# All layer norms of an eight-layer kernel: in two halves with loops written out, and every fourth tile normalised by ScalarE

## What is computed

```
def _layernorm(x, axis=-1, eps=1e-05):
    m = jnp.mean(x, axis=axis, keepdims=True)
    v = jnp.var(x, axis=axis, keepdims=True)
    return (x - m) / jnp.sqrt(v + eps)

x = x + _L0_attn_ref(_layernorm(x, axis=-1), ...)   # delta net
x = x + _L0_ffn_ref(_layernorm(x, axis=-1), ...)    # sine feed-forward
...                                                 # six more of this form
x = x + _L3_ffn_ref(_layernorm(x, axis=-1), ...)    # routed experts
```

## Time and profile before

| | |
|---|---|
| median of 3 runs | 3606.04 us (3604.13 to 3606.18) |
| the profiled execution | 3612.15 us, span 3610.3 us |
| busy share of the span | TensorE 69%, VectorE 50%, ScalarE 36%, GpSimd 20% |
| mean granted clock of TensorE | 0.771 of full speed |

### The profile page before, as it was taken

The page is one execution under the profiler, slowest core; times in us unless marked ns, Lnnn a source line. Parts: engine busy times, 40 slices in busy tenths (PEclk is TensorE's granted clock), DMA queues, the critical chain, the costliest instruction groups (busy, mean ns, idle before and its releaser), DMA issues.

```text
span 3610.3 us, 65131 instructions
## 1 busy us (share of the span) xinstructions
PE 2505.6 (69%) x20692; PEld 1381.9 (38%) x20744; DVE 1809.9 (50%) x3541; ACT 1295.6 (36%) x2627; POOL 717.2 (20%) x1299
## 2 busy tenths in 40 slices
PE   2330695767676766675499999544898998988954
PEld 1220463445455545342234444331333333333433
DVE  2115255642222222366366666354777777777353
ACT  1111010522222221101156566322666666666512
POOL 3551132024444444002001111010000000000012
PEclk8565555867777686686599999665999999999766
DMA  1122421000000000000411110005111111111000
GB/s 30 42 53 49 98 61 40 0 6 0 0 0 0 0 0 0 7 0 13 143 28 30 27 27 22 3 16 139 29 29 31 27 31 30 28 31 27 10 14 23
DMA packets 129382, 103.26 MB, mean 29 GB/s; under 512 B 52254, under 2 KB 108967, under 8 KB 129002
## 3 DMA queue, kind: packets, MB, share of 16 engines
q1 hardware_dynamic: 129258, 101.55, 10.9%
HBM read 58.96 MB, written 41.94 MB: 28 GB/s over the span
## 4 chain that ended last, share of the span: by engine, by line
PE 50%; DVE 16%; POOL 11%; issue 11%; SPq 4%; ACT 4%; DVEq 2%; DMA 1%; POOLq 0%; ACTq 0%; PEldq 0%
PE psum L1811 9%; PE psum L1823 7%; PE psum L1800 6%; PE psum L1835 5%; SPq L1737 3%; DVE ba_blockmax L2029 2%; DVE X L1195 2%; PE psum L586 1%; POOL dn_ss L745 1%; POOL dn_vscale L746 1%; PE psum L1341 1%; PE psum L1328 1%; PE psum L1359 1%; PE psum L382 1%; ACT ba_pt L1899 1%
## 5 line engine op out<-in xcount | busy, mean ns | idle before, releaser
L2029 DVE TENSOR_REDUCE ba_blockmax<-psum 128x16 f32<-128x1024 f32 x512 | 609.2, 1221 | 200.3 <-PE psum L1800 196.9
L1899 ACT ACTIVATE ba_pt<-psum 128x512 f32<-128x512 f32 x1024 | 542.1, 601 | 286.5 <-PE psum L1811 286.4
L1800 PE MATMUL psum<-ba_ks,ba_qs 64*128 64x512 bf16 x1024 | 362.8, 433 | 45.4 <-DMA ba_ks<-ba_kstk 31.1
L1811 PE MATMUL psum<-ba_qs,ba_ks 64*128 64x512 bf16 x1024 | 335.4, 403 | 82.9 <-DVEq L59 51.5
L2031 DVE TENSOR_REDUCE sa_negmax<-psum 128x1 f32<-128x1024 f32 x256 | 304.5, 1221 | 164.6 <-PE psum L1800 164.2
L1899 ACT ACTIVATE sa_pt<-psum 128x512 f32<-128x512 f32 x512 | 268.7, 602 | 201.0 <-PE psum L1811 124.2
L1823 PE MATMUL psum<-ba_pt,ba_vh 128*32 128x512 f32 x2048 | 306.1, 673 | 0.0
L1800 PE MATMUL psum<-sa_ks,sa_qs 96*128 96x512 bf16 x512 | 200.1, 396 | 52.0 <-DMA sa_ks<-sa_kstk 31.3
L1811 PEld LDWEIGHTS psum<-ba_qs,ba_ks 64*128 64x128 bf16 x1024 | 80.2, 95 | 394.9 <-issue 366.0
L1811 PE MATMUL psum<-sa_qs,sa_ks 128*128 128x512 bf16 x460 | 175.4, 385 | 22.0 <-DVEq L59 19.4
L1942 POOL CAST ba_mparts<-ba_negmax 128x8 bf16<-128x8 f32 x64 | 12.2, 191 | 821.5 <-DVE ba_negmax L2044 821.5
(11 more groups left out here) (468 smaller groups left out, 4543.8 us busy)
## 6 DMA issues: line engine op xcount, KB each, us to landing
ba_qs<-ba_qstk SPq DMA_DIRECT2D x128, 96.0 KB, 2.1
ba_ks<-ba_kstk SPq DMA_DIRECT2D x128, 96.0 KB, 2.2
sa_qstk<-sa_pq SPq DMA_DIRECT2D x48, 128.0 KB
sa_kstk<-sa_pk SPq DMA_DIRECT2D x48, 128.0 KB
sa_qs<-sa_qstk SPq DMA_DIRECT2D x32, 192.0 KB, 2.6
sa_ks<-sa_kstk SPq DMA_DIRECT2D x32, 192.0 KB, 2.7
ba_qstk<-ba_pq SPq DMA_DIRECT2D x48, 128.0 KB, 2.3
ba_kstk<-ba_pk SPq DMA_DIRECT2D x48, 128.0 KB, 2.3
```

Of the source, the lines that this page charges most:

```text
L1800: last = nc.tensor.matmul(bank(2 * slot + h), qs[b][0:KP, :].rearrange("p (a r) -> p r a", r=NTB)[:, r, :], ks[b][0:KP, h * HALF:(h + 1) * ...
L1811: nc.tensor.matmul(bank(4 + slot), ks[b][K0:P, x_ * P:(x_ + 1) * P], qs[b][K0:P, h * HALF:(h + 1) * HALF], start=True, stop=True).then_inc ...
L1899: nc.scalar.activation(pt[2 * x_ + h][:, :], bank(4 + slot), ACT.Exp, scale=SCALE).then_inc(pt_in, 1)
L2029: ins = nc.vector.tensor_reduce(blockmax[g][:, r, :], src.rearrange("p (n s) -> p n s", s=BLOCK), AXX, ALU.max, negate=True)
```

## The change

Only layer_norm is changed. The 32 tiles are treated as two halves of 16: VectorE takes statistics, aggregates and adds EPS for one half, tells GpSimd, and goes on with the other; GpSimd computes a power of 16 columns for each half (twice each in sa). All loops of the norm over tiles and groups, on VectorE, TensorE and ScalarE, are written out, with constant addresses. In front of groups 0 and 4 VectorE waits for the root of the half and computes shift = -mean * rstd for it. Of each group VectorE normalises three tiles and ScalarE the fourth, as Identity with scale rstd and bias shift, one group ahead of its copies. TensorE waits for each tile of VectorE by itself (ready) and for ScalarE's (ready_a).

```diff
--- before.py
+++ after.py
@@ -120,6 +120,8 @@
     nc = k.nc
     tag = f"{tag}_norm"
     ready = [k.sem(f"{tag}_ready{g}") for g in range(2)]
+    ready_a = [k.sem(f"{tag}_ready_a{g}") for g in range(2)]
+    shift_in = k.sem(f"{tag}_shift_in")
     turned = [k.free_sem(f"{tag}_turned{g}") for g in range(2)]
     written = [k.free_sem(f"{tag}_xt{g}") for g in range(2)]
     var_in, root_out = k.sem(f"{tag}_var"), k.sem(f"{tag}_root")
@@ -131,71 +133,92 @@
     root = k.sb(f"{tag}_root_buf", [P, NT], ctx=ctx)
     rstd = k.sb(f"{tag}_rs", [P, NT], ctx=ctx)
     tmp = k.sb(f"{tag}_ln_tmp", [P, 2, NT], ctx=ctx)
+    shift = k.sb(f"{tag}_shift", [P, NT], ctx=ctx)
+    MINE = GROUP - 1
     layer = k.layers
+    halves = [slice(h * NT // 2, (h + 1) * NT // 2) for h in range(2)]
 
     def vector(v):
         k.start(v, layer)
         c = Chain(v, own)
-        with v.Fori(0, NT // 8) as i:
-            for n in range(8):
-                c.do(nc.vector.bn_stats(stats[:, bass.ds(i * 8 + n, 1), :], k.X[:, bass.ds(i * 8 + n, 1), :]))
-            c.restart()
-        for n in range(NT):
-            c.do(nc.vector.bn_aggr(mv[:, n, :], stats[:, n, :]))
-        c.sync()
-        nc.vector.tensor_scalar(tmp[:, 0, :], mv[:, :, 1], EPS, None, ALU.add).then_inc(var_in, 1)
-        v.wait_ge(root_out, 1)
+        for at in halves:
+            for n in range(at.start, at.stop):
+                c.do(nc.vector.bn_stats(stats[:, n, :], k.X[:, n, :]))
+            c.sync()
+            for n in range(at.start, at.stop):
+                c.do(nc.vector.bn_aggr(mv[:, n, :], stats[:, n, :]))
+            c.sync()
+            nc.vector.tensor_scalar(tmp[:, 0, at], mv[:, at, 1], EPS, None, ALU.add).then_inc(var_in, 1)
         if twice:
-            c.step(nc.vector.tensor_tensor(tmp[:, 0, :], rstd[:, :], rstd[:, :], ALU.mult))
-            c.step(nc.vector.tensor_tensor(tmp[:, 1, :], tmp[:, 0, :], mv[:, :, 1], ALU.mult))
-            nc.vector.tensor_scalar(tmp[:, 0, :], tmp[:, 1, :], EPS, None, ALU.add).then_inc(var_in, 1)
-            v.wait_ge(root_out, 2)
-            c.step(nc.vector.tensor_tensor(rstd[:, :], rstd[:, :], root[:, :], ALU.mult))
+            for h, at in enumerate(halves):
+                v.wait_ge(root_out, h + 1)
+                c.step(nc.vector.tensor_tensor(tmp[:, 0, at], rstd[:, at], rstd[:, at], ALU.mult))
+                c.step(nc.vector.tensor_tensor(tmp[:, 1, at], tmp[:, 0, at], mv[:, at, 1], ALU.mult))
+                nc.vector.tensor_scalar(tmp[:, 0, at], tmp[:, 1, at], EPS, None, ALU.add).then_inc(var_in, 1)
+        for g in range(NG):
+            i, z = g // 2, g % 2
+            if g % (NG // 2) == 0:
+                h = 2 * g // NG
+                v.wait_ge(root_out, (3 if twice else 1) + h)
+                if twice:
+                    c.step(nc.vector.tensor_tensor(rstd[:, halves[h]], rstd[:, halves[h]], root[:, halves[h]], ALU.mult))
+                if twice:
+                    v.wait_ge(own, c.n)
+                nc.vector.scalar_tensor_tensor(shift[:, halves[h]], mv[:, halves[h], 0], -1.0, rstd[:, halves[h]], ALU.mult,
+                                               ALU.mult).then_inc(shift_in, 1)
+            v.wait_ge(turned[z], i + 1)
+            for n in range(MINE):
+                t = g * GROUP + n
+                nc.vector.tensor_scalar(xn[z][:, n, :], k.X[:, t, :], mv[:, t, 0:1], rstd[:, t:t + 1],
+                                        ALU.subtract, ALU.mult).then_inc(ready[z], 1)
         c.restart()
-        with v.Fori(0, NG // 2) as i:
-            for g in range(2):
-                v.wait_ge(turned[g], i + 1)
-                for n in range(GROUP):
-                    t = i * 2 * GROUP + g * GROUP + n
-                    last = nc.vector.tensor_scalar(xn[g][:, n, :], k.X[:, bass.ds(t, 1), :], mv[:, bass.ds(t, 1), 0],
-                                                   rstd[:, bass.ds(t, 1)], ALU.subtract, ALU.mult)
-                    if n < GROUP - 1:
-                        c.do(last)
-                c.sync()
-                last.then_inc(ready[g], 1)
-            c.restart()
 
     def tensor(t):
         k.start(t, layer)
-        with t.Fori(0, NG // 2) as i:
-            for g in range(2):
-                t.wait_ge(ready[g], i + 1)
-                t.wait_ge(written[g], i + 1)
-                for n in range(GROUP):
-                    last = nc.tensor.transpose(k.psum[:, g, n * P:(n + 1) * P], xn[g][:, n, :], k.ident[:, :])
-                last.then_inc(turned[g], 1)
+        for g in range(NG):
+            i, z = g // 2, g % 2
+            t.wait_ge(written[z], i + 1)
+            for n in range(GROUP):
+                if n < MINE:
+                    t.wait_ge(ready[z], MINE * i + n + 1)
+                else:
+                    t.wait_ge(ready_a[z], i + 1)
+                last = nc.tensor.transpose(k.psum[:, z, n * P:(n + 1) * P], xn[z][:, n, :], k.ident[:, :])
+            last.then_inc(turned[z], 1)
 
     def scalar(a):
         k.start(a, layer)
         if affine_in is not None:
             a.wait_ge(*affine_in)
-        with a.Fori(0, NG // 2) as i:
-            for g in range(2):
-                a.wait_ge(turned[g], i + 2)
-                dst = k.XT[:, bass.ds(i * 2 * GT + g * GT, GT)]
-                if place is not None:
-                    nc.scalar.copy(place(i, g), k.psum[:, g, :].rearrange("p (c t) -> p c t", t=P // B)).then_inc(written[g], 1)
-                elif affine is None:
-                    nc.scalar.copy(dst, k.psum[:, g, :]).then_inc(written[g], 1)
-                else:
-                    nc.scalar.activation(dst, k.psum[:, g, :], ACT.Identity, scale=affine[0],
-                                         bias=affine[1]).then_inc(written[g], 1)
+
+        def normalise(g):
+            i, z = g // 2, g % 2
+            t = g * GROUP + MINE
+            a.wait_ge(shift_in, 1 + 2 * g // NG)
+            a.wait_ge(turned[z], i + 1)
+            nc.scalar.activation(xn[z][:, MINE, :], k.X[:, t, :], ACT.Identity, scale=rstd[:, t:t + 1],
+                                 bias=shift[:, t:t + 1]).then_inc(ready_a[z], 1)
+
+        normalise(0)
+        for g in range(NG):
+            i, z = g // 2, g % 2
+            if g < NG - 1:
+                normalise(g + 1)
+            a.wait_ge(turned[z], i + 2)
+            dst = k.XT[:, g * GT:(g + 1) * GT]
+            if place is not None:
+                nc.scalar.copy(place(i, z), k.psum[:, z, :].rearrange("p (c t) -> p c t", t=P // B)).then_inc(written[z], 1)
+            elif affine is None:
+                nc.scalar.copy(dst, k.psum[:, z, :]).then_inc(written[z], 1)
+            else:
+                nc.scalar.activation(dst, k.psum[:, z, :], ACT.Identity, scale=affine[0], bias=affine[1]).then_inc(written[z], 1)
 
     def gpsimd(p):
         k.start(p, layer)
         for q in range(2 if twice else 1):
-            p.wait_ge(var_in, q + 1)
-            nc.gpsimd.tensor_tensor((root if q else rstd)[:, :], tmp[:, 0, :], k.mhalf[:, 0:NT], ALU.pow).then_inc(root_out, 1)
+            for h, at in enumerate(halves):
+                p.wait_ge(var_in, 2 * q + h + 1)
+                nc.gpsimd.tensor_tensor((root if q else rstd)[:, at], tmp[:, 0, at], k.mhalf[:, 0:NT // 2], ALU.pow).then_inc(root_out, 1)
 
     k.add(vector=vector, tensor=tensor, scalar=scalar, gpsimd=gpsimd)
     return written
```

## The result

| | before | after |
|---|---|---|
| median | 3606.11 us (3604.13 to 3615.8, 4 runs) | 3471.18 us (3468.66 to 3473.79, 4 runs) |
| profiled execution, span | 3612.15, 3610.3 us | 3468.66, 3466.8 us |
| busy TensorE, VectorE, ScalarE, GpSimd | 69, 50, 36, 20% | 72, 51, 38, 21% |

The account below looks back on a forecast made before the run. No engine bounds the kernel; the eight layer norms, 272.03 us, lie fully on the path as successive stages. Savings of 79.7 (six norms), 13.6 (ba) and 11.9 (sa) sum to 105.2 us off the median 3606.04: 3501 us, range 3486 to 3533.

Parts of the forecast that it names:

- Statistics written out: VectorE's statistics in each norm, without loops: 4.62 us a half, 9.24 us for both halves.
- A power doesn't hold VectorE's tiles: VectorE writes tiles beside GpSimd's second power without delay; waiting for that power's end would cost 2.9 us a norm.
- The cover: Second power lies under the first groups' tiles; groups 4 to 7 suffer only if its root comes after 13.1 us or so.
- The tiles' period: Tiles, transposes and copies on three engines: 1.0 us a group, between 0.92 and today's 1.54.
- dn's one table load: dn's norm loads ScalarE's table once, not on four passes, 1.28 us a load; group 0 is delayed by 0.8 us.
- sa: sa's norm: groups after 0 to 2 wait until memsets end at 24.9 us; 32.2 us long, 11.9 less.
- I take the later stages to run as now … some us either way: Stages behind the norms keep their times and are costed at nothing, though TensorE's granted clock changes behind the norms.
- the prediction's own last sign of being wrong: Stretches between the norms that differ from today's by more than some us would show the prediction wrong.
- ba: ba's norm: memsets interleave with tiles over groups 3 to 7, 2.5 us more; 21.25 us long, 13.6 saved.
- Rival 3: Moved code makes other loops' restarts dearer; 3523 us at 0.5 us a pass; chance 0.03 slower, 0.02 the same.
- Rival 2: Tiles don't speed up: semaphores round three engines keep 1.45 us a group in eight norms; 3526 us, chance 0.13.
- Rival 1: A GpSimd power holds VectorE's tiles: six norms lose 2.9 us each, sa and ba save less; 3528 us, chance 0.22.

Follow-up runs that it names:

- extra_power: Changed kernel with one more 16-column power on a spare tile in GpSimd's queue ahead of the last power; 3498.33 us, ratio 0.9677.
- before_again: The kernel before the change, unedited, run and profiled again on the experiments' chips; 3613.32 us, ratio 0.9998.
- after_again: The changed kernel, unedited, run and profiled again, against the kernel before on the same chip; 3473.80 us, ratio 0.9604.

## Why the forecast was wrong, step by step

| step | forecast | measured |
|---|---|---|
| first tile after the first bn_stats | 9.45 | 9.10 |
| first tile to end of the last copy | 9.3 | 8.08 |
| six norms together save | 79.7 | 89.3 |
| ba saves | 13.6 | 15.0 |
| sa saves | 11.9 | 17.3 |
| between the norms | 0 | 21.9 |
| sum | 105.2 | 143.5 |

The last column is the difference of the two profiled executions (3612.15 and 3468.66). One was 6 over its median, the other 2.5 under, so the medians give 134.9, and 139.0 in the later pair. Of the 21.9, 0.3 lies ahead of dn's first bn_stats.

The mechanism was right, and no rival came true. Three terms of the sum failed: the tiles' period, taken as 1.0; sa's second half, let wait for the memsets' end; and the later stages, put at nothing. The norms saved 16.4 us more than forecast, and the low end had allowed for 8.5; the rest of the program gave 13 by the medians, and it had allowed for 6. So about 8 of the 15 us under the range are the norms' and 7 the later stages'.

- *Statistics written out*: right, 4.62 a half forecast and 4.61 measured, and the first power at 4.78, the second at 9.19 against 4.8 and 9.4. The rest of the 0.35 is that shift and tile each start 0.08 us behind the instruction ahead, not 0.2.
- *A power doesn't hold VectorE's tiles*: right, and shown (twelve tiles in 3.35 us, nearly all of it beside a power of 3.06). L885 was the right row to go by, and it told more than I read in it: by the same section of the Trainium skill a form with two inputs in SBUF contends with GpSimd work that reads SBUF, as a power does, and its 0.35 us inside the power was its usual time (0.352 is the median of 32). The Trainium skill's rule (SBUF — State Buffer, Who interferes with whom), by which the first tiles would end at 12.35, doesn't fit the power. It fits the memsets where the two engines take turns (no tile over 1.2 us); a hung tile waited for the whole row of ten or eleven memsets, not for one.
- *The cover*: my limit of 13.1 was too late. At 12.25 there is at most 0.2 us of slack, as extra_power shows. Here it cost nothing.
- *The tiles' period*: this term failed. The floor of 0.88 for ScalarE, from the copy, the pointer operands and the SBUF source, was exact: 0.88, with a tile of 0.49 to 0.50. I took 1.0 instead, with no engine's work behind it. The last group is quicker still, since no tile stands between the last two copies (1.11 us for both). Together 1.2 us a norm, 7.3 in six.
- *dn's one table load*: right; 1.28 us ahead of ScalarE's first tile, and the norm 1.0 longer than the others (18.13).
- *sa*: what failed is "the rest I let wait to the end, as this layer shows it today". The row is of a tile that came behind a memset. In the changed kernel the tiles come first. 26.77 is near the 28.2 that I had for turns.
- *"I take the later stages to run as now … some us either way"*: this term failed, and the prediction's own last sign of being wrong came true. Stretches that the diff doesn't touch gave 13 us by the medians, 21.9 in the first pair of profiles and 15.4 in the second (before_again and after_again): 9.1 and 7.7 from dn's to sf's norm, 5.0 and 3.3 in ba's own stretch, 2.8 and 2.6 in tt's. Of dn's, 5.0 and 6.0 are TensorE's stalls between instructions. 1.0 is the four products right behind dn's norm, 1.13 us in all nine kernels written out where they took 2.10 in the four with loops. The other 1 to 3 have no cause that I could show. The 1.8 and 1.7 that sf's and rf's stretches gave in the first pair didn't repeat (-1.0 and -0.2). sf's follows the granted clock over it: 101.9 us at 0.90 of full speed, 105.8 at 0.82, 110.0 at 0.78.
- *ba*: near, but not by the interleaving alone: its norm is 34.84 or 38.16 us before and 19.83 or 24.39 after, so the saving is 10 to 18 by which executions are compared.
- *Rival 3* had the right place, code that moves, and the wrong sign; its mechanism, dearer loop passes, no run shows. *Rival 2* is out: 0.83 to 0.99 us a group on the mean of a plain norm in all kernels written out but extra_power, which has one long gap. *Rival 1* would have cost 3.1 a plain norm, and 24 to 27 us in all.

Left open: why some stretches gain. tt's is 713.7 to 714.3 us long in the four profiles with loops in the norm and 710.8 to 713.3 in the nine without, ba's 1025.0 to 1025.3 and 1015.9 to 1023.3. Their granted clock is the same (0.73 to 0.76, and 0.86 to 0.88, over both kinds), so it isn't the clock. Open, too, is why a tile that comes first hangs in some executions.

## What to carry to other kernels

When a loop of short instructions on the path is written out, cost the loop's own share first: it was 8.5 us of a plain norm's 15 here, the overlap 5.4. Where an estimate gives one engine's work for a step and nothing else stands in the way, take that number rather than a rounder one above it. And give a change to a program's code a price of its own in stages that it doesn't touch, in both directions: a pad of no-effect waits in a profiled run shows whether stalls move with it, here by 4 us.

Where GpSimd writes large tiles beside VectorE's work, try to start it behind that work: 4.7 to 9.3 us in two norms here, for a wait.

## What the runs showed of the hardware

- Bursts of 32x32 products stand still for 1.1 to 6.9 us at a time without a wait in the profile, 22.0 and 22.2 us in dn's stretch before and 12.4 to 17.2 in the kernels written out. The stalls come behind the same products in each execution, 127, 128 or 255 apart where they follow each other, and move when code ahead of them is added.
- Ten or eleven memsets on GpSimd (0.2 to 1.2 us each) and VectorE's tensor_scalar either take turns, with tiles of 0.4 to 1.2 us, or one tile of 0.34 hangs for 5.8 to 7.3 us. In turns the memsets are longer too (1.09 for 0.95).
- A power of 16 columns takes 2.90 us, and 3.06 with tiles beside it: GpSimd is held a little, VectorE is not.
- An Identity with scale and bias from two SBUF columns on a 128x128 tile takes ScalarE 0.49 to 0.50 us.
